# Graph network, two layers: source columns copied on chip for the fourth tile of a quarter of the groups

## What is computed

```python
# layer 0
m = relu(concat([x[dst], x[src], edge_attr, u[batch[dst]]]) @ W1.T + b1)
agg = segment_sum(m, dst, 6250)
x = layernorm(x + relu(concat([x, agg, u[batch]]) @ W2.T + b2))
# layer 1
h = relu(concat([x[src], x[dst], edge_attr]) @ msg_w1 + msg_b1)
agg = segment_sum(h @ msg_w2 + msg_b2, dst, 6250) / counts
x = layernorm(x + relu(concat([x, agg]) @ upd_w1 + upd_b1) @ upd_w2 + upd_b2)
```

## Time and profile before

| | |
|---|---|
| median of 3 runs | 3929.26 us |
| profiled execution (its time and its span) | 3929.8 us |
| instructions | 45222 |
| mean granted TensorE clock | 0.56 of full speed |
| PE busy | 3229.0 us, 82% |
| weight loads (PEld) busy | 2975.7 us, 76% |
| POOL busy | 2960.2 us, 75% |
| DVE busy | 1583.8 us, 40% |
| ACT busy | 590.4 us, 15% |
| DMA | 563.18 MB, mean 143 GB/s |

### The profile page before, as it was taken

One profiled execution on the slowest core, in us unless ns is written; L12 is line 12 of the kernel. 1 busy time (PEld: TensorE's weight loads), 2 busy tenths in 40 slices (PEclk: granted clock), 3 DMA queues, 4 the chain that ended last, 5 costly groups with the idle time before them and its releaser, 6 DMA issues.

```text
span 3929.8 us, 45222 instructions
## 1 busy us (share of the span) xinstructions
PE 3229.0 (82%) x16881; PEld 2975.7 (76%) x16881; DVE 1583.8 (40%) x3640; ACT 590.4 (15%) x1017; POOL 2960.2 (75%) x3156
## 2 busy tenths in 40 slices
PE   6988888888788888888878888878888888888887
PEld 6877777777777777777778777777777777777776
DVE  6533334343444444444543333333433333333333
ACT  1211111111111111111111111111111111111111
POOL 7777777777777777777777777777777777777776
PEclk7755555565655556665665555555555555555556
DMA  7644444444444444445454444444444444444443
GB/s 261 200 138 134 135 136 143 132 133 139 148 139 149 149 149 147 147 147 154 131 158 135 133 131 124 135 139 136 139 136 141 139 142 137 140 135 141 142 142 100
DMA packets 257760, 563.18 MB, mean 143 GB/s; under 512 B 131254, under 2 KB 151713, under 8 KB 232572
## 3 DMA queue, kind: packets, MB, share of 16 engines
q1 hardware_dynamic: 132824, 332.20, 25.4%
q0 software_dynamic: 100032, 205.00, 19.8%
q10 hardware_dynamic: 24676, 23.01, 1.7%
HBM read 537.29 MB, written 22.66 MB: 142 GB/s over the span
## 4 chain that ended last, share of the span: by engine, by line
POOL 70%; issue 23%; DMA 4%; DVE 2%; PE 2%; ACT 0%; SPq 0%; POOLq 0%; DVEq 0%
POOL Qr L319 70%; DMA Qr<-tabQ,srcE 3%; DVE BIG L1405 1%; PE bank L1137 0%; DMA srcE<-in_srcL 0%; DVE BIG L1302 0%; PE bank L1119 0%; PE bank L1092 0%; DVE BIG L1392 0%; DMA tabQ<-BIG 0%; DVE BIG L1400 0%; PE bank L1051 0%; PE bank L1045 0%; DVE AC L609 0%; POOL Qr L325 0%
## 5 line engine op out<-in xcount | busy, mean ns | idle before, releaser
L319 POOL DMA_INDIRECT Qr<-tabQ,srcE x3094 | 2925.3, 945 | 942.9 <-issue 933.2
L1137 PE MATMUL bank<-BIG 128*128 128x42 f32 x6252 | 1379.0, 396 | 143.6 <-ACT BIG L1287 141.1
L1119 PE MATMUL bank<-wall,BIG 128*128 128x128 f32 x6252 | 1473.0, 410 | 19.1 <-DMA BIG<-tabP 19.1
L1137 PEld LDWEIGHTS bank<-BIG 128*128 128x128 f32 x6252 | 1307.5, 308 | 207.6 <-ACT BIG L1287 201.5
L1302 DVE TENSOR_TENSOR BIG<-bank,BIG 126x512 bf16<-126x512 f32 x782 | 539.3, 690 | 2264.7 <-DMA Qr<-tabQ,srcE 2254.8
L1119 PEld LDWEIGHTS bank<-wall,BIG 128*128 128x128 f32 x6252 | 1311.5, 309 | 23.8 <-issue 23.8
L1287 ACT ACTIVATE BIG<-BIG 128x512 f32<-128x512 f32 (+1 forms) x782 | 492.1, 629 | 3229.1 <-DVE BIG L1405 3220.4
L1124 PE MATMUL bank<-BIG 126*128 126x128 bf16 x3126 | 490.2, 295 | 506.5 <-DVE BIG L1302 396.7
L1124 PEld LDWEIGHTS bank<-BIG 126*128 126x128 bf16 x3126 | 342.0, 135 | 639.0 <-DVE BIG L1302 455.9
L1405 DVE TENSOR_TENSOR BIG<-bank,Qr 128x512 f32<-128x512 f32 (+1 forms) x782 | 532.7, 681 | 41.2 <-PE bank L1124 25.3
L1392 DVE TENSOR_TENSOR BIG<-bank,relE 128x168 f32<-128x168 f32 x782 | 252.6, 323 | 3.5 <-DMA Qr<-tabQ,srcE 3.5
(11 more groups left out here) (137 smaller groups left out, 609.9 us busy)
## 6 DMA issues: line engine op xcount, KB each, us to landing
BIG<-in_eaT SPq DMA_DIRECT2D x194, 1024.0 KB, 5.4
BIG<-in_dstR SPq DMA_DIRECT2D x194, 504.0 KB
Qr<-tabQ,srcE POOLq DMA_INDIRECT x3094
BIG<-tabP SPq DMA_DIRECT2D x526, 31.5 KB
tabP<-BIG ACTq DMA_DIRECT2D x22, 384.0 KB, 3.1
tabQ<-BIG ACTq DMA_DIRECT2D x17, 256.0 KB, 5.2
X<-in_xN SPq DMA_DIRECT2D x1, 3136.0 KB, 16.8
tabE<-BIG ACTq DMA_DIRECT2D x11, 256.0 KB, 2.3
```

The costliest lines, as they stand in the source:

```text
L319: e.indirect_dma_start(Q[0:p, i % R_Q, j, :], None, table[:, :], bass.IndirectOffsetOnAxis(ap=srcE[0:p, g, j:j + 1], axis=0)).then_inc(f_q ...
L1119: e.matmul(bank[i % R_C][:, j * D:(j + 1) * D], f_eaT[:, k % R_EA, (g % LQ * J + j) * P:(g % LQ * J + j + 1) * P], wc[l], start=(j == 0), ...
L1137: last = e.matmul(sums[:, 0:W], M[:, i % R_M, j, :], S[:, hot(i), j, :], start=(j == 0 and first_of(i)), stop=(j == n - 1 and last_of(i)))
```

## The change

In some groups only three tiles are gathered. The fourth tile's source part is made on chip: one engine copies, for each of its 128 edges, the source's column of XT into one column of a tile XC, and TensorE multiplies XC with wq into the fourth quarter of the group's bank. The relu of that quarter then reads the bank.

There are two copiers (COPIERS). ScalarE serves the groups 10, 16, 22 ... (every sixth), VectorE the groups 17, 29, 41 ... (every twelfth). In layer 0 that is 64 and 31 tiles, in layer 1, where the first two groups' steps of each copier are left out, 63 and 30. The 128 columns of a tile are spread over six or twelve group steps, ahead of the group that uses them: about 21 or 11 copies a step. For each step the node numbers are loaded from colI into registers (values_load), and each copy has its address from a register. Both engines do their copies at the end of a group step.

XT now has to keep the old x until the last column of layer 0 is copied. So in layer 0 the new columns of x go into AC[:,0] (whose sums are used up by then), q1 reads them there, and `xt_move` on ScalarE brings them to XT later: units 0 to 10 in the last seven group steps of layer 0, the last three at the first step of layer 1 (MOVES). VectorE clears AC[:,0] after that (`clear`), instead of in `second`.

The core of the diff:

```diff
+MOVES = [(0, NG - 7 + u // 2) for u in range(NU - 3)] + [(1, 0)] * 3
+MOVED = 2
+COPIERS = ((6, 10), (12, 17))
...
+R_X = 2
...
+        def gathered(i):
+            return tiles(i % NG) - (col_tile(i) is not None)
...
-                for j in range(tiles(g)):
+                for j in range(gathered(i)):
...
+            e.dma_start(colI[0:len(COL_ROWS), :], a["srcC"]).then_inc(s_bas, 16)
...
+                        if col_tile(i) is not None:
+                            h, c = col_tile(i)
+                            e.wait_ge(s_col[h], COPIERS[h][0] * (c + 1))
+                            e.matmul(bank[i % R_C][:, (J - 1) * D:J * D], XC[h][:, c % R_X, :], wq[l], start=False, stop=False)
...
-                e.copy(XT[:, b * P:(b + n) * P], bank[unit_bank(0, "x1t", u)][:, 0:n * P]).then_inc(u_tc, 1)
+                e.copy(AC[:, 0, b * P:(b + n) * P], bank[unit_bank(0, "x1t", u)][:, 0:n * P]).then_inc(u_tc, 1)
...
+            def columns(l, g):
...
+                c, row, lo, hi, new = col_piece(0, l, g)
+                if new and c >= R_X:
+                    e.wait_ge(v_C, col_group(0, c - R_X) + 1)
+                if new and c == len(TAKEN[0][0]):
+                    e.wait_ge(s_mv, NU)
+                _, at = nc.values_load_multi_w_load_instructions(
+                    colI[row:row + 1, lo:hi], engines=[mybir.EngineType.Activation], min_val=0, max_val=N - 1,
...
+                for x in range(lo, hi):
+                    last = e.copy(XC[0][:, c % R_X, x:x + 1], XT[:, bass.ds(at[x - lo], 1)])
+                last.then_inc(s_col[0], 1)
...
+                        last = e.activation(m, m, ACT.Relu)
+                        if col_tile(i) is not None:
+                            last = e.activation(M[:, i % R_M, J - 1, :], bank[i % R_C][:, (J - 1) * D:J * D], ACT.Relu)
+                        last.then_inc(v_rl, 1)
+                        columns(l, g)
```

More of the change, by code:

```diff
@@ L100, with col_tile, col_group, col_piece @@
 LAST = BASE[-1]
+MOVES = [(0, NG - 7 + u // 2) for u in range(NU - 3)] + [(1, 0)] * 3
+MOVED = 2
+COPIERS = ((6, 10), (12, 17))
+TAKEN = [[[n * per + lead for n in range(NG) if n * per + lead < NG - 2 and n * per >= (0, MOVED)[l]] for l in range(2)]
+         for per, lead in COPIERS]
+COL_ROW = [sum(len(TAKEN[x][0]) for x in range(k)) for k in range(len(COPIERS))]
+COL_ROWS = [i for t in TAKEN for i in t[0]]
+R_X = 2
+def col_tile(i):
+    l, g = divmod(i, NG)
+    for k in range(len(COPIERS)):
+        if l < 2 and g in TAKEN[k][l]:
+            return k, len(TAKEN[k][0]) * l + TAKEN[k][l].index(g)
+    return None
+def col_group(k, c):
+    return TAKEN[k][0][c] if c < len(TAKEN[k][0]) else NG + TAKEN[k][1][c - len(TAKEN[k][0])]
+def col_piece(k, l, g):
+    per, lead = COPIERS[k]
+    n, q = divmod(g, per)
+    if n * per + lead not in TAKEN[k][l]:
+        return None
+    return col_tile(l * NG + n * per + lead)[1], COL_ROW[k] + n, q * P // per, (q + 1) * P // per, q == 0
 ROWS = [2 + SPACED * (c - UPFRONT) for c in range(NC)]
@@ L307, in tiles @@
             return -(-VALID // P) if g == NG - 1 else J
+        def gathered(i):
+            return tiles(i % NG) - (col_tile(i) is not None)
         def q_count(i):
-            return 16 * sum(tiles(x % NG) for x in range(i % R_Q, i + 1, R_Q))
+            return 16 * sum(gathered(x) for x in range(i % R_Q, i + 1, R_Q))
         def gathers(e, l, g0, g1, table):
@@ L1044, in q1 @@
                 for k in range(n):
-                    last = e.matmul(bank[o][:, k * D:(k + 1) * D], XT[:, (b + k) * P:(b + k + 1) * P], wq[1], start=(k == 0), stop=(k == n - 1))
+                    last = e.matmul(bank[o][:, k * D:(k + 1) * D], AC[:, 0, (b + k) * P:(b + k + 1) * P], wq[1], start=(k == 0), stop=(k == n - 1))
                 last.then_inc(u_q, 1)
@@ L1050, in q1 @@
                 for k in range(n):
-                    last = e.matmul(bank[3][:, k * D:(k + 1) * D], XT[:, (b + k) * P:(b + k + 1) * P], wp[1], start=False, stop=(k == n - 1))
+                    last = e.matmul(bank[3][:, k * D:(k + 1) * D], AC[:, 0, (b + k) * P:(b + k + 1) * P], wp[1], start=False, stop=(k == n - 1))
                 last.then_inc(p_c, 1)
@@ L1285, in fast_scalar @@
                         e.wait_ge(v_tt, i + 1)
[L1286 to L1287 removed]
+                        m = M[:, i % R_M, 0:gathered(i), :].rearrange("p j d -> p (j d)")
+                        last = e.activation(m, m, ACT.Relu)
[3 more added lines that the diff above has]
+                        columns(l, g)
         def fast_vector(e):
@@ L1372, in rows_lo, with columns @@
                 e.tensor_tensor(fP3[:, c % R_U, 0:n, 2 * D:3 * D], row_bank(c), fP3[:, c % R_U, 0:n, D:2 * D], ALU.subtract).then_inc(p0["lo"], 1)
+            def columns(l, g):
+                if col_piece(1, l, g) is None:
+                    return
+                c, row, lo, hi, new = col_piece(1, l, g)
+                if new and c >= R_X:
+                    e.wait_ge(v_C, col_group(1, c - R_X) + 1)
+                if new and c == len(TAKEN[1][0]):
+                    e.wait_ge(s_mv, NU)
+                _, at = nc.values_load_multi_w_load_instructions(
+                    colI[row:row + 1, lo:hi], engines=[mybir.EngineType.DVE], min_val=0, max_val=N - 1,
+                    skip_runtime_bounds_check_because="the source of an edge, which is a node")
+                for x in range(lo, hi):
+                    last = e.tensor_copy(XC[1][:, c % R_X, x:x + 1], XT[:, bass.ds(at[x - lo], 1)])
+                last.then_inc(s_col[1], 1)
             stored(e, s_tabQ[0])
@@ L1403, in fast_vector @@
                             e.wait_ge(f_q[i % R_Q], q_count(i))
-                        n = tiles(g - 1)
+                        n = gathered(i)
                         e.tensor_tensor(M[:, i % R_M, 0:n, :].rearrange("p j d -> p (j d)"), bank[i % R_C][:, 0:n * D],
@@ L1450, in fast_vector @@
                             mean(u)
+                    if g < NG:
+                        columns(l, g)
         def flag(e):
```

35 lines of the change are left out of this document (29 added, 6 removed).

## The result

The changed kernel takes 4696.07 us (median of 4 runs, 4692.4 to 4712.07) where the kernel before takes 3929.47 (4 runs, 3928.97 to 3930.61). The ratio is 1.196, 95% interval 1.194 to 1.198: 19.6% slower, where the forecast was 3696.5 us and 5.9% faster. The change does what it says. The 188 gathers are gone; something else has become the bound.

A forecast was written before the change was run, and what follows sets the result against it. POOL's gathers were taken to bound the kernel: 3929.8 - 188 x 1.249 (234.8) = 3695.0, 3694.5 against the median, plus 2 us for the shared port, gives 3696.5 us, 5.9% faster; range 3688 to 3810.

The forecast's parts named there:

- What bounds the kernel before: GpSimd's (POOL's) gathers bind at 1.249 us each, start to start; 188 fewer save 234.8 us.
- ACT's step: ScalarE per group: 21.3 copies at 0.11, index load 0.35, relu 0.63, together 3.3 of 4.70 us, 71%.
- the prediction's own formula: ScalarE's time per group: 21.3 times a column's price, plus 0.35 us load and 0.63 us relu.
- ACT becomes the bound: Rival: ScalarE's column copies without overlap, 0.205 us each, make 5.35 us a group and 4244 us; chance 0.10.
- the formula behind the 4244: 762 ScalarE groups at 5.35 us, plus 20 groups at 4.99, 53.6 us before the first relu and 14 after the last.
- ACT takes over beyond 0.175 us a column: ScalarE's threshold per column copy: (4.70 - 0.63 - 0.35)/21.3 = 0.175 us, against 0.11 forecast.
- DVE's step: VectorE per group: 2.03 us of existing work, 10.7 copies at 0.12, load 0.34, together 3.65 of 4.70 us, 78%.
- PE: TensorE's 188 more 128x128 products at 0.47 us add 88 us, hidden: 3317 of 3695 us busy, 90%.
- Moved work: x transposed through AC, ScalarE's later moves to XT, the delayed clearing, and start and boundary effects: 0 us.
- The shared port: VectorE's column copies and GpSimd's gathers may lock each other out: 2 us taken, 0 to 32 kept.
- the port starves POOL: Rival: gathers wait for the rest of a whole batch of VectorE's columns, 508 us more, 4200 us; chance 0.03.
- A part of the gain is lost: Rival: ScalarE's column at 0.18 us, or PE stalls behind late relus; 3833 us, range 3740 to 3920; chance 0.12.

The follow-up runs named there:

- the floor kernel: Changed kernel without loads of node numbers, each piece of columns written by one copy of XT's first columns: 3697.74 us, ratio 0.9405 to the kernel before.
- the aligned kernel: Changed kernel with pieces of columns starting at multiples of four (20, 20, 24 on ACT, 8 or 12 on DVE): 3703.39 us, ratio 0.942 to the kernel before.
- that with more tiles: The aligned kernel with 226 tiles taken instead of 188, every fifth group for ACT and every tenth for DVE: 3667.11 us, ratio 0.931 to the kernel before.

## Why the prediction was wrong

*What bounds the kernel before*: right. 188 gathers fewer bring 188 x 1.249 = 234.8 us when nothing else is in the way: the floor kernel gains 234.1.

*ACT's step*: wrong, and this is the step that failed. The load was counted "in full" with 0.35 us. The rows it came from were loads of up to four numbers, 341 ns, and the prediction took the price of an instruction for that of any load of the kind. The load here brings 21 numbers. By the very same row, at up to four numbers a go, six goes would have been 2 us, and one number a go, which the row didn't exclude, 7 us. Measured were 1.52, 4.66 and 4.88, mean 3.69, ten times the term; it was 3.3 us too small in a step that had 1.4 us to spare. The Trainium skill (Runtime: NRT & Kernel Launch, section Instruction fetch mechanics) has a price that the prediction didn't draw on: it gives some 200 ns a register for loads of registers, in bulk too, there from HBM. By it, 21.3 numbers are an estimated 4.3 us; the loads here are from SBUF, and the rows agree for those that aren't aligned (0.22 us a number) and differ for the aligned ones (0.06). The other terms were close: a column 0.092 us (0.11 forecast; 0.187 of duration, of which the next overlaps half), the address 37 ns, the relu 0.62. With the measured load, the prediction's own formula gives 3.69 + 21.3 x 0.094 = 5.7 us with the relu beside the load, and with the steps read above (5.80) 762 x 5.80 + 168 = 4588 us. The rest to 4694, 106 us, is for the most part work of ACT for which the formula has no term, the copies, activations and DMA issues of the node updates and of the tables: in the trace the 146 steps from relu to relu that hold such work take 6.64 us on the mean and the other 635 take 5.76, which is 128 us more.

*The rival "ACT becomes the bound"*: the mechanism and the sign were right, and so was its place: POOL released by DVE's add, hardly any waiting of ACT. Its cause was wrong: it hung on the column's price (0.205), which wasn't it, and was given 0.10. That all of the doubt was put into the copy and none into the load is what made the range too narrow: 3688 to 3810 had no bound for the load at all. (The 0.189 us a column at which the kernel would be as fast as before comes out as 0.186 by the formula behind the 4244: (3929.3 - 167.4)/762 = 4.94 us, less 0.98, over 21.3.)

*ACT takes over beyond 0.175 us a column*: the same sum, turned round, leaves 4.70 - 0.63 - 21.3 x 0.11 = 1.73 us for the load. The aligned load, 1.3 to 1.5, is under it; the unaligned one is not. Both sides were shown by runs.

*DVE's step*: same error, 0.34 against 2.10 us for its load. With aligned pieces its load averages (4 x 0.62 + 8 x 0.87)/12 = 0.79 us, and with 2216.8/782 = 2.83 of instructions the step is 3.6 us, where 3.65 stood.

*PE*: 188 products more hide. They are busy 104.6 us in the aligned kernel, where 88 stood. PE as a whole is 83% busy there, not 90%, at a mean granted clock of 0.62 of full speed in place of 0.56.

*Moved work*: at nothing, right: the floor kernel has it all and takes 3697.7 us, where 3694.5 stood; of the 3.2 us, 2.5 are between the kernel before in its session (3931.81) and in the forecast (3929.26).

*The shared port*: 2 us were taken, 0 to 32 kept. (By the prediction's own reading a copy of 0.15 us less 0.13 delays a gather by 0.02, not 0.04, so the upper end was 16.) The gathers are busy 2748.7 us in the aligned kernel, 945.9 ns each; in the kernel before 2925.3/3094 = 945.5. That makes 1 us. The Trainium skill's rule (SBUF, section Who interferes with whom), that such a copy of DVE and a GpSimd operation block each other, has no price that shows for copies of one column: 7808 of them went by beside POOL.

*The rival "the port starves POOL"*: out, by the same row. *"A part of the gain is lost"*: in the aligned kernel 5.7 us of the gain, in that with more tiles another 5.6, of 47.5.

## What to carry to other kernels

Price an instruction by its operands, not by its name: a load that fetches 21 numbers isn't a load that fetches four, and a row for the small one is a lower bound of it. A time on a queue that is no busy time ("issue" in front of an instruction) still holds up everything behind it, so the queue instructions of a new step are to be added up like the others. Let what is read into registers in a batch start at a multiple of four numbers; the trace tells within one kernel whether it matters, if the durations of one line fall into groups that follow the position.
